# Graph network on one core: sums over edges from counted cells and indirect gathers to fixed cells of 32 slots, gathered and added by one-hot matrices

## The reference

```python
# pass 0, gated cell
msg = x[src] @ W_msg.T + b_msg + edge_embed[type]
messages = segment_sum(msg, dst)
x = layernorm(x + gru_cell(messages, x))
# passes 1 to 3, three layers (widths 128 -> 256 -> 128)
h = x[dst] + (ea @ enc_w + enc_b)          # concatenated in layers 2 and 3
agg = segment_sum(h, src)                  # a self loop for each node as well
h = relu(bn(agg @ w1 + b1)) @ w2 + b2      # relu between layers
out = layernorm(x + h)
```

## Time and profile before

| | us |
|---|---|
| median of 3 runs | 9222.99 |
| lowest and highest | 9198.98, 9262.44 |
| span of the profiled execution, first to last instruction | 6865.3 |

### The profile page before, as it was taken

The page is one execution under the profiler, slowest core; times in us unless marked ns, Lnnn a source line. Parts: engine busy times, 40 slices in busy tenths (PEclk is TensorE's granted clock), DMA queues, the critical chain, the costliest instruction groups (busy, mean ns, idle before and its releaser), DMA issues.

```text
span 6865.3 us, 82277 instructions
## 1 busy us (share of the span) xinstructions
PE 5821.5 (85%) x28969; PEld 2842.2 (41%) x29103; DVE 3274.0 (48%) x8044; ACT 1341.4 (20%) x2496; POOL 5114.9 (75%) x4958
## 2 busy tenths in 40 slices
PE   3278888778874777766799999999999999999999
PEld 1133333333332443333344544444454444445444
DVE  6477777666664766766444444422222222222222
ACT  1044444444441222222111111100000000000000
POOL 3777777777777777776677777777777777777775
PEclk9999999999996777777899999999999999999999
DMA  6199999999995333333788778888888778787876
GB/s 236 39 235 251 249 245 250 247 252 249 245 254 143 109 107 105 108 103 93 235 245 248 232 244 248 246 264 244 251 241 251 241 244 270 241 243 238 246 238 188
DMA packets 1387715, 1479.05 MB, mean 215 GB/s; under 512 B 818563, under 2 KB 1125316, under 8 KB 1387308
## 3 DMA queue, kind: packets, MB, share of 16 engines
q1 hardware_dynamic: 1174812, 1124.63, 57.6%
q0 software_dynamic: 212496, 349.08, 19.8%
HBM read 1024.47 MB, written 281.76 MB: 190 GB/s over the span
## 4 chain that ended last, share of the span: by engine, by line
PE 53%; POOL 7%; DVE 3%; issue 3%; DMA 1%; ACT 1%; SPq 0%; DVEq 0%; ACTq 0%; POOLq 0%
PE ps L2566 34%; PE ps L2536 6%; POOL BIG L2622 5%; PE ps L2502 2%; POOL GL L2640 2%; PE ps L2504 1%; PE ps L2417 1%; PE ps L2489 1%; PE ps L2418 1%; DVE BIG L1936 1%; PE ps L2510 1%; PE ps L2511 1%; PE ps L2456 1%; PE ps L2419 1%; DMA RECL<-rec_q 0%
## 5 line engine op out<-in xcount | busy, mean ns | idle before, releaser
L2640 POOL DMA_INDIRECT GL<-h_gathered,IDXA x2646 | 2707.8, 1023 | 872.0 <-issue 776.5
L2566 PE MATMUL ps<-MS,HP 128*128 128x512 bf16 (+1 forms) x11700 | 2715.1, 376 | 20.4 <-DMA MS<-counts 15.9
L2607 POOL DMA_INDIRECT rec_q<-BIG x1563 | 1569.4, 1004 | 598.0 <-issue 473.5
L2566 PEld LDWEIGHTS ps<-MS,HP 128*128 128x128 bf16 x11700 | 1132.7, 98 | 1251.8 <-issue 121.9
L2357 PE MATMUL ps<-MT,XPS 128*128 128x512 bf16 x3780 | 1081.0, 396 | 271.4 <-ACT MT L2158 212.9
L2622 POOL DMA_INDIRECT BIG<-x_parts,SRCq x739 | 833.0, 1127 | 227.0 <-issue 223.7
L2158 ACT CAST MT<-ps 128x512 bf16<-128x512 f32 x1274 | 711.6, 589 | 1108.0 <-DMA BIG<-MT 601.6
L2013 DVE TENSOR_REDUCE ROW<-ps 128x128 f32<-128x384 f32 x294 | 163.0, 554 | 1504.1 <-PE ps L2536 1504.1
L2357 PEld LDWEIGHTS ps<-MT,XPS 128*128 128x128 bf16 x3822 | 369.5, 100 | 763.6 <-ACT MT L2158 328.8
L2536 PE MATMUL ps<-GL,SL 128*128 128x384 bf16 (+1 forms) x2646 | 593.9, 334 | 31.0 <-DVE SL L1979 26.8
L2343 PE MATMUL ps<-BIG 128*128 128x512 bf16 x1182 | 462.5, 392 | 84.4 <-DVE BIG L1800 74.7
(11 more groups left out here) (203 smaller groups left out, 4717.6 us busy)
## 6 DMA issues: line engine op xcount, KB each, us to landing
MS<-counts SPq DMA_DIRECT2D x936, 512.0 KB
counts<-BIG SPq DMA_DIRECT2D x312, 512.0 KB, 3.6
XPS<-x_parts SPq DMA_DIRECT2D x168, 384.0 KB
GL<-h_gathered,IDXA POOLq DMA_INDIRECT x2646
rec_q<-BIG POOLq DMA_INDIRECT x1563
rec_q<-BIG SPq DMA_DIRECT2D x44, 490.0 KB, 15.2
HTI<-h_cols SPq DMA_DIRECT2D x72, 256.0 KB, 5.6
RECL<-rec_q SPq DMA_DIRECT2D x24, 520.0 KB, 6.4
```

Of the source, the lines that this page charges most:

```text
L2566: got = t.matmul(bank[:, 0:w].rearrange("p (b c) -> p b c", c=P), HP[:, d, part, :], MS[:, i % MR, 0:x.nb, d % MB, :], start=d + part == 0 ...
L2607: g.indirect_dma_start(out=RAd, out_offset=bass.IndirectOffsetOnAxis(ap=POSI[:, c:c + 1], axis=0), in_=RECA[q % 3][:, c - a, :], in_offset ...
L2640: g.indirect_dma_start(out=GL[:, r % LR, i, 0:3 * P], out_offset=None, in_=HGd[lay], in_offset=bass.IndirectOffsetOnAxis(ap=IDXA[:, a + i: ...
```

## The change: what it does

Every pass now sums in one way. The 98 blocks of `dst` times 98 blocks of `src` make cells, and each cell gets 32 slots (`RS = 32`); an edge goes to the next free slot of its cell. Edges over 32 in a cell (190 of the 200,000 in these inputs) go to three short "spill" lists of up to 128 edges each. Four cells make a tile of 128 slots; a pass has 98 output blocks times 25 tiles, 2,450 tiles, the four passes 9,800.

For a tile, `gather_tensor` issues four matrix products. Each has a one-hot of 128 nodes by 32 slots as stationary operand (`GX`), placed on its own quarter of PE's columns (`tile_position=(0, 32j)`), and the 384 columns of one node block as moving operand; together they put the features of 128 slots in a PSUM bank. ACT (three tiles of four) or DVE (the fourth) copies them to SBUF as bfloat16 (`EV`). `scatter_tensor` then multiplies with a one-hot of 128 slots by 128 output nodes (`CX`) and adds up over the 25 tiles of the block. In `stage_tensor` PE alternates: the gather of tile t, then the scatter of tile t - 4, and so on. There are four banks for gathered tiles. The node features of all blocks stay in SBUF (`XP`). Tables of the slots' nodes are stored in DRAM and broadcast to all partitions (`row_sync`, three DMAs for each output block).

The sort phase (`first_phase_*`) works on one destination block at a time: 18 columns of 128 edges, one-hots on DVE, prefix sums on PE, ranks summed by ACT's accumulator, then `table_tensor` and `columns_tensor` make the tables. POOL writes only the attributes of the edges to their slots, 1,568 indirect DMAs; there are no gathers by DMA left except nine for the spill lists and nine of their features. After pass 1 a phase of its own sums the attributes (`attrs_*`), and another does layer 0's perceptron for all nodes (`first_mlp_*`). Gone are the count matrices, their transposes and their reads, the gathers and their one-hots. Inputs `idx3`, `ea2` and `b2r` are added (rows of src, dst and type for each edge; attributes in edge order; biases). The general way for inputs that don't fit is kept; it isn't run here.

The diff replaces nearly all of `program`. Its core, removed loops first:

```diff
-    def rows_tensor(t, x, g):
...
-        for i in range(LT):
-            got = t.matmul(bank[:, 0:w], SL[:, r % LR, i, :], GL[:, r % LR, i, 0:w], start=at + i == 0,
-                           stop=at == KQ - 1 and i == LT - 1, skip_group_check=True)
-        got.then_inc(*row_sum.inc())
...
-    def layer_tensor(t, k):
...
-        for d in range(BD):
...
-            for part in range(3):
-                got = t.matmul(bank[:, 0:w].rearrange("p (b c) -> p b c", c=P), HP[:, d, part, :],
-                               MS[:, i % MR, 0:x.nb, d % MB, :], start=d + part == 0, stop=False, skip_group_check=True)
...
+    def gather_tensor(t, st, tile):
+        o, s = divmod(tile, SG)
+        gt = st.tile0 + tile
+        if tile >= 4:
+            copied_tensor(t, st, tile - 4)
+        elif st.i:
+            copied_tensor(t, STAGES[st.i - 1], NTILE - 1 - (NTILE - 1 - tile) % 4)
+        gq = st.chunk0 + NCK * o + s // CT
+        if s % CT == 0:
+            t.wait_ge(g_hot.sem, gq + 1)
+        if o == 0:
+            t.wait_ge(parts.sem, st.group0 + s + 1)
+        at = P * (s % CT)
+        gx = GX[gq % GR]
+        for j in range(blocks(s)):
+            got = t.matmul(PS[tile % 4][RS * j:RS * (j + 1), 0:W3], gx[:, at + RS * j:at + RS * (j + 1)], XP[:, 4 * s + j, :, :],
+                           start=True, stop=True, tile_position=(0, RS * j))
+        got.then_inc(*gat.inc())
...
+    def scatter_tensor(t, st, tile):
+        o, s = divmod(tile, SG)
+        gt, go = st.tile0 + tile, st.outer0 + o
+        copied_tensor(t, st, tile)
+        if s == 0 and go >= 2:
+            t.wait_ge(red.sem, go - 1)
+        m, w = RS * blocks(s), st.width
+        bank = PS[4 + go % 2][:, 0:w]
+        got = t.matmul(bank, CX[0:m, gt % CR, :], EV[0:m, gt % ER, 0:w], start=s == 0, stop=False,
+                       skip_group_check=True)
+        if gt % 2:
+            got.then_inc(*sct.inc())
+        if s < SG - 1:
+            return
+        t.wait_ge(cs_hot.sem, go + 1)
+        if not st.first:
+            t.matmul(bank, IDQ[:], XP[:, o, :, :], start=False, stop=False, skip_group_check=True)
+        mine = [third_of(o)] if st.first else range(3)
+        for th in mine:
+            got = t.matmul(bank, CS[:, go % 2, 0 if st.first else th, :], EVS[:, th, 0:w], start=False,
+                           stop=th == mine[-1], skip_group_check=True)
+        got.then_inc(*sums.inc())
...
+    def stage_tensor(t, st):
+        steps = XSTEPS if st.first else LSTEPS
+        for k in range(LOOPS):
+            if 1 <= k <= NBT:
+                t.wait_ge(c_hot.sem, st.batch0 + k)
+            for i in range(4):
+                if 4 * k + i < NTILE:
+                    gather_tensor(t, st, 4 * k + i)
+                if k and 4 * (k - 1) + i < NTILE:
+                    scatter_tensor(t, st, 4 * (k - 1) + i)
+            for step, n in steps.get(k, []):
+                if st.first:
+                    node_tensor(t, step, n)
+                else:
+                    layer_tensor(t, st, step, n)
...
+    def chunk_vector(v, st, q):
+        o, c = divmod(q, NCK)
+        gq = st.chunk0 + q
+        h = next(i for i in range(3) if CT * c < ROWCUT[i + 1])
+        gr = st.row0 + 3 * o + h
+        if CT * c == ROWCUT[h]:
+            v.wait_ge(row_in[gr % RR].sem, 16 * (gr // RR + 1))
+        if gq >= GR:
+            v.wait_ge(gat.sem, last_tile(gq - GR) + 1)
+        w = min(P * CT * (c + 1), RS * NB) - P * CT * c
+        at = P * (CT * c - ROWCUT[h])
+        v.tensor_scalar(GX[gq % GR][:, 0:w], ROW[gr % RR][:, at:at + w], PID1[:, 0:1], None,
+                        ALU.is_equal).then_inc(*g_hot.inc())
...
+    def columns_vector(v, st, k):
+        tiles = st.tiles(k)
+        last = st.tile0 + tiles[-1]
+        if last >= ER:
+            v.wait_ge(sct.sem, (last - ER) // 2 + 1)
+        for t in tiles:
+            o, s = divmod(t, SG)
+            m = RS * blocks(s)
+            if st.first:
+                if s == 0 and o % 4 == 0:
+                    v.wait_ge(tx_in[o // 4 % 2].sem, 16 * (o // 8 + 1))
+                col = TXR[o // 4 % 2][0:m, o % 4, 0, s:s + 1]
+            else:
+                col = COLL[0:m, s, o:o + 1]
+            got = v.tensor_scalar(CX[0:m, (st.tile0 + t) % CR, :], IOQ[0:m, 0 if st.first else 1, :], col, None, ALU.is_equal)
+        if st.first:
+            for o in sorted({t // SG for t in tiles}):
+                own = [t for t in tiles if t // SG == o]
+                a, n, s = own[0] % ER, len(own), own[0] % SG
+                got = v.tensor_tensor(EV[:, a:a + n, W3:W3 + 10], IOTA[:, 1:11].unsqueeze(1).broadcast_to([P, n, 10]),
+                                      TXR[o // 4 % 2][:, o % 4, 1, s:s + n].unsqueeze(2).broadcast_to([P, n, 10]), ALU.is_equal)
+        got.then_inc(*c_hot.inc())
...
+    def evac_vector(v, st, k):
+        for t in st.tiles(k):
+            gt = st.tile0 + t
+            if t % 4 >= OWN:
+                v.wait_ge(gat.sem, gt + 1)
+                if gt >= ER:
+                    v.wait_ge(sct.sem, (gt - ER) // 2 + 1)
+                v.tensor_copy(EV[:, gt % ER, 0:W3], PS[t % 4][:, 0:W3]).then_inc(*evac_v.inc())
...
+    def evac_scalar(s, st, k):
+        for t in st.tiles(k):
+            gt = st.tile0 + t
+            if t % 4 < OWN:
+                s.wait_ge(gat.sem, gt + 1)
+                if gt >= ER:
+                    s.wait_ge(sct.sem, (gt - ER) // 2 + 1)
+                s.copy(EV[:, gt % ER, 0:W3], PS[t % 4][:, 0:W3]).then_inc(*evac_a.inc())
...
+    def spill_block_vector(v, st, o):
...
+        for th in ([third_of(o)] if st.first else range(3)):
+            got = v.tensor_scalar(CS[:, go % 2, 0 if st.first else th, :], IOTA[:], float(P * o),
+                                  SPF[:, th, 1:2] if st.first else SPF[:, th, 0:1], ALU.add, ALU.is_equal)
...
+    def ranks_tensor(t, g, c):
...
+            t.matmul(bank, NTRIB, oh[:, c - 2, 0:n, :], start=False, stop=False, skip_group_check=True)
...
+            t.matmul(bank, ONEH, oh[:, c - 1, 0:n, :], start=c == 1, stop=False, skip_group_check=True)
+        t.matmul(bank, TRIB, oh[:, c, 0:n, :], start=c == 0, stop=True, skip_group_check=True).then_inc(*rank.inc())
+    def rank_scalar(s, g, c):
...
+        for i in range(n):
+            got = s.activation(PS[5 + c % 2][:, NB * i:NB * (i + 1)], PS[c % 2][:, NB * i:NB * (i + 1)], ACT.Relu, bias=NBIG,
+                               accum_out=RNK[g % 2][:, i, c:c + 1])
...
+    def values_vector(v, g):
...
+        for h in range(n // 2):
...
+            v.tensor_tensor(EQ, IOH.unsqueeze(1).unsqueeze(1).broadcast_to([P, 2, WC, RS]),
+                            RNK[b][:, hh, :].unsqueeze(3).broadcast_to([P, 2, WC, RS]), ALU.is_equal).then_inc(*dve.inc())
...
+            v.tensor_tensor(RV[h][:, :, :, 0:RS], EQ, V1[b][:, hh, :].unsqueeze(3).broadcast_to([P, 2, WC, RS]),
+                            ALU.mult).then_inc(*dve.inc())
+            v.tensor_tensor(RV[h][:, :, :, RS:2 * RS], EQ, V2[b][:, hh, :].unsqueeze(3).broadcast_to([P, 2, WC, RS]),
+                            ALU.mult).then_inc(*rv.inc())
...
+    def attrs_vector(v):
...
+        for pc in range(2 * SG):
...
+            for q in range(7):
...
+                for i in range(7):
...
+                    got = v.tensor_scalar(CTT[0:m, 7 * (w % 2) + i, :].bitcast(F32R), IOT1[0:m, :], COLL[0:m, g, b:b + 1], None,
+                                          ALU.is_equal)
...
+            for i in range(7):
...
+                                      ALU.is_equal)
...
+    def attrs_tensor(t):
...
+                for i in range(7):
...
+                    got = t.matmul(PS[b // TB][:, TW * (b % TB):TW * (b % TB) + TW], CTT[0:m, 7 * (w % 2) + i, :].bitcast(F32R),
+                                   RT[pc % 2][0:m, 7 * q + i, :].bitcast(F32R), start=g == 0 and b % TB == 0, stop=False,
...
+            for i in range(7):
...
+                got = t.matmul(PS[b // TB][:, TW * (b % TB):TW * (b % TB) + TW], CTT[:, 7 * (w % 2) + i, :].bitcast(F32R),
...
+    def row_sync(y, st, o):
+        for h in range(3):
...
+            y.dma_start(ROW[gr % RR][:, 0:b - a], table[o:o + 1, a:b].broadcast_to([P, b - a])).then_inc(*row_in[gr % RR].inc(16))
+    def quick_gpsimd(g):
...
+        for q in range(NQ):
...
+            for c in range(columns(q)):
...
+                g.indirect_dma_start(out=RECd, out_offset=bass.IndirectOffsetOnAxis(ap=IXC[:, b, c:c + 1], axis=0),
+                                     in_=EAC[:, b, c, :], in_offset=None).then_inc(*scat[b].inc(16))
...
+    def quick_tensor(t):
+        weights_tensor(t)
+        first_phase_tensor(t)
+        t.wait_ge(weights_dve.sem, 10)
+        t.wait_ge(bias_in.sem, 16)
+        t.wait_ge(coll.sem, SG)
+        t.wait_ge(cxi.sem, SG)
+        t.wait_ge(spilled.sem, 3)
+        stage_tensor(t, STAGES[0])
+        nodes_over(t)
+        stage_tensor(t, STAGES[1])
+        attrs_tensor(t)
+        first_mlp_tensor(t)
```

(108 more changed lines are left out.)

2605 lines of the change are left out of this document (1243 added, 1362 removed).

## The result

The changed kernel takes 10,310 us, median of four runs, against 9,243 for the kernel before beside it: ratio 1.115, interval 1.110 to 1.119, slower. The forecast was 10,700 (7,500 to 12,900). Its span is 10,306.6 us, so only 3 us lie outside it, where the prediction had 2,358.

What follows compares the result with a forecast made beforehand. PE was taken to bound the layers, with POOL a second bound. PE's 6,501 us for four passes plus 1,805 for separate phases gave a span of 8,306; plus 2,358 outside it, 10,664, say 10,700 us (7,500 to 12,900).

Steps and rivals of the forecast that it cites:

- the signs named in the prediction: Profile after: PE near 100% in passes, a tile every 0.57 us, DVE near 60%, ACT near half, sort ending near 760.
- sort: Sort phase at the start: 677 us on DVE, ACT's rank sums 500 to 860; with the start taken as 760 us.
- a tile on PE: Four gathers and one addition on PE: 0.402 us staggered plus half of each of two 0.164 us tails, 0.566 us.
- four passes: PE's work in the passes: 9,800 tiles, 5,547 us, plus gated cell, perceptrons, self loops and spill lists, 6,501 us.
- attribute sums: Phase after pass 1: 2,744 float32 one-hots on DVE at 0.2 us, 549, with subtractions 605 us.
- layer 0's perceptron: Layer 0's perceptron in a phase alone: 29 steps of some 8.6 us, 250 us.
- I carry 2,358 over unchanged.: Timed median 9,223 us less profiled span 6,865: the unexplained 2,358 us were added unchanged to the new span.
- Rival 4: Time outside the span shrinks with fewer indirect DMAs, 0.48 us each: 756 us remain, forecast becomes 9,062; chance 0.3.
- POOL "costed at nothing, hidden": POOL's 1,568 attribute scatters, 2,174 us, run beside sort, pass 0 and pass 1, so add no time.
- Rival 2: Each change of arrangement on PE leaves the whole tail open: 0.730 us a tile, time 12,271 us; chance 0.2.
- rival 3: PE's quarters run one after another: 0.81 us a tile, time 13,055 us; chance 0.15.
- Rival 1: Changes of arrangement cost nothing: 0.324 us a tile, DVE bounds, 8,412 us; or staggered 0.402, 9,057; chance 0.3 together.

Runs made afterwards that it cites:

- the runs of four: Changed kernel with four gathering tiles, then four adding tiles in a row: 7,075 us where the kernel before takes 6,885, 9,055 us where it takes 9,068.
- The last experiment: Four-tile order plus, against that order alone, bf16 attribute sums, four groups in flight and subtraction moved mid-half-group: 8,750 us, ratio 0.958 to the kernel before.

## Why the prediction held, and where it did not

The direction and the range were right, and the median lies 4% under the forecast. The sum of the span, 8,306 us, is that of the kernel without scatters (8,306.0), but that equality is luck: passes and sort, forecast 297 us too long, stand against attribute sums, perceptron and gaps, forecast 297 too short. What was added to the sum was wrong in kind. Of the signs named in the prediction, the tile, PE's, DVE's and ACT's shares held where no scatters run; the sort ended at 1,160 us and not near 760, and in the dead stretches PE fell to 8% busy and its clock to 0.50.

The rows down to the sum of the span are measured without scatters.

| step | forecast, us | measured, us |
|---|---|---|
| sort | 760 | 755 |
| a tile on PE | 0.566 | 0.5445 |
| four passes | 6,501 | 6,209 (1,657 + 1,413 + 1,561 + 1,578) |
| attribute sums | 605 | 801 |
| layer 0's perceptron | 250 | 338 |
| splitting, fills, drains | 190 | 203 (the gaps between the stages and the 18 us at the end) |
| sum of the span | 8,306 | 8,306 |
| POOL's scatters | 0 | 2,001 |
| outside the span | 2,358 | 3 |

**"I carry 2,358 over unchanged."** This step failed. The profile shown of before has the span that it has on a chip on which it takes 6,885 us (6,865.3 and 6,864.6); its timed runs are those of a chip on which it takes 9,243. The difference lies inside the span, goes with semaphore updates that land late while POOL issues indirect DMAs, and had to be worked out for the new kernel by its own scatters. Rival 4 had the right suspect, the indirect DMAs, but spread the 2,358 us over all 4,948 of before, 0.48 each. After pays 1.26 to 1.28 for each of 1,568, before about 0.45 for each of 4,948 (2,222 us), a third of that. Why before pays less is not shown. That it has many products to a hand-over between engines, and after one tile every 0.54 us, is a guess, and the runs of four, with a hand-over for four tiles, pay 1.26 all the same. The two errors, 2,001 in place of 0 and 3 in place of 2,358, nearly cancel, so the close number is luck.

**POOL "costed at nothing, hidden".** Failed on the second kind of chip by 2,001 us, and in one detail on any: the three gathers of spilled rows wait for the end of pass 0, and 480 or so scatters are queued behind them. Moving the three gathers behind them changed the time by 0.8% only: a scatter costs much the same wherever it stands. On the first kind of chip the cover holds, as the fours show.

**The tile.** 0.566 was 0.402 and half of two tails. Both terms were off and the errors nearly cancel: the quarters start 3 ns apart, so 0.324 and not 0.402, and a change costs 0.110 and not 0.082. The prediction's reason for the half, that some of the tail is delivery of results, is not shown by any run. The Trainium skill (TensorEngine Tiling (Array Packing), Tiling Modes, Key Properties) says that a change of the tiling mode drains TensorE. The trace agrees that a change costs time, 0.110 us, two thirds of the 0.164 us tail; the runs of four, with a quarter of the changes, take 7,075 us on the chip on which the kernel that alternates took 8,334, without scatters. Rival 2 (whole tails) and rival 3 (serial quarters) fell with the same rows. Rival 1's tile came true only where the arrangement never changes.

**Passes.** 9,800 x 0.5445 = 5,336, 211 below the 5,547. The other 81 us lie in what stands beside the tiles (node work, perceptrons, self loops, spill lists); they were not parted.

**The attribute sums.** The term counted DVE's work alone, 605, and DVE is indeed busy 609 of the 801 us. What it left out is the queue of one after another: the next half group's copy waits for PE, the subtraction for the copy, and all one-hots for the subtraction. The last experiment took this chain away, with cheaper one-hots, and shortened the phase to 498.

**Layer 0's perceptron.** 338 us and not 250, since the term counted PE's work alone. PE is busy 214 us of the 338, and waits for the loads of the stored sums, as this row of the changed kernel shows:

```profile
L2637 PE MATMUL ps<-IDN,REST 128*128 128x128 f32 x196 | 47.4, 418 | 115.3 <-DMA REST<-sums_q 113.5 <-ACT EAC L2353 1.0 <-ACT AR L2361 0.7
```

**What the change costs on each kind of chip.** On the second kind 1.115 to 1.138. On the first kind after itself was not run. The kernel without scatters stands at 1.209 there, and the updates that would stall it are not late there in the fours, so after should be near 1.21; this stays an estimate. With that, the kernel loses some 1,450 us (8,334 - 6,885), most of it PE's, and on the second kind wins 200 to 400 of it back, because before is some 2,200 to 2,400 us slower there and after 2,001.

What stays open: what makes a chip one of the second kind, and where an update waits. No run looks inside that. Each chip was measured on one occasion, so it is not shown either that the kind belongs to the chip and not to the occasion.

## What to carry to other kernels

Between products on quarters of the array and on all of it, count 0.110 us for each change (measured at full clock with 384 columns): gather and add in runs, not in turn. Before a difference between timed runs and a profiled span is carried over as a constant, compare the two on one chip; if "another core or an unknown queue" holds a large part of the chain on a one-core kernel, look at how late updates land beside POOL's indirect DMAs. There the new kernel pays POOL's whole issue time for each indirect DMA, in turn or in fours, and before a third of it.
